# A macaron block on one Trainium2 core: max scores three steps further from their transpose, exponentials four steps later, two of twelve runs joined

## The chip, the cores and the metric

One core of one Trainium2 chip runs the whole program. The core has a matrix engine (TensorE, PE in the profile; PEld is its loading of weights), a vector engine (VectorE, DVE), a scalar engine (ScalarE, ACT), a general engine (GpSimd, POOL) and a queue that issues transfers (SyncE, SP). The metric is the device time of one execution in microseconds, and the median of three runs is compared.

## The reference

Two batches of 1024 tokens with 512 channels pass through half a feed-forward layer with ternary weights, an attention layer of 16 heads of width 32, and half a feed-forward layer again:

```python
x = x + 0.5 * _L0_ffn_ref(_layernorm(x, axis=-1), weight, bias, ln_gamma, ln_beta)
x = x + _L0_attn_ref(_layernorm(x, axis=-1), w_q, w_k, w_v, w_o)
x = x + 0.5 * _L0_ffn_ref(_layernorm(x, axis=-1), weight, bias, ln_gamma, ln_beta)
# attention, for each head: q and k with rotary embedding
scores = where(mask, q @ k.T * SCALE, -inf)     # causal in blocks of 64, in effect
ctx = softmax(scores) @ v
out = ctx @ w_o.T
```

With a dilation of one block every block at or before the query's is allowed, so the mask is causal in blocks of 64.

## The kernel before

The 16 heads of a batch are taken four at a time, so that there are 8 groups of four heads (`ALL`). The middle of the kernel is one long list of steps `k`, and every engine runs the same list in its own order of instructions. 48 steps (`STEPS`) belong to one group, 12 steps (`A_UNITS`) to one head. In a step TensorE issues, in this order, at most:

- one exponential's score product (L920, "B unit"): keys on the partitions, one of 12 key steps (`st`, called key step below) of one of the four heads. Key step 0 to 3 have 512, 384, 256, 128 columns, 4 to 8 have 512, and 9 to 11 have 384, 256, 128. ScalarE takes the exponential of it into `probs` (L609), which has room for four key steps. There are two banks for B units, so that B unit u waits until the exponential of u-2 is done (L919).
- one max product (L939, "A unit"): queries on the partitions, one of 12 units of a head, number 0 to 11, with 128, 256, 384, 512, 512, 128, 512, 256, 512, 384, 512, 512 columns. VectorE reduces it to its maximum (L815). There are three banks, so that an A unit waits until the reduction of the unit three before it is done (L937).
- one or two of the 12 projection products of a later group (L956): at k mod 12 from 0 to 9, two of them at 4 and at 9, none at 10 and 11. After them ScalarE copies the projection out (L602, at k mod 12 = 10), GpSimd turns it by the rotary angles in four instructions (two at L502, then L505 and L507), ScalarE makes the high half (L623, eight steps after the projection's last), GpSimd the low half (L511), and SP writes both out to `spread` and reads them back into `qst` or `kst` (L398 to L409). In the last groups output products (L884) and the second feed-forward layer (L864 to L874) stand in their place, in the first the values' products (L993).
- where k mod 4 is 3, a "run": four products with ones (L1045, the sums of the exponentials of one key step, five steps behind its first B unit, `SUM_LAG`) and four with the values (L1055, the key step before that one, nine steps behind, `PV_LAG`), in fp32 and in four parts of the array side by side.
- once a head the transpose of the head's max parts (L1063).

When the last A unit of a head (number 11) is reduced, VectorE makes the "max parts" of the head in three small instructions, each waiting for the one before: L825 takes the smaller of two columns sets, L827 a scaled fp16 copy, L828 what the copy leaves out. L1063 transposes them on TensorE `MAX_PLACE` steps after unit 11, in a bank of the three A banks (`max_bank`), ScalarE copies the result one step later (L617), and SP writes it into `qst` two steps later (L414). The next A unit of that bank waits for the copy (`s_mrows`, L933), and the two before it wait one unit deeper (L935). With `A_START` = 10 unit 0 stands at k mod 12 = 10 and unit 11 at 9, and the transpose at 11, behind the run there. With `B_START` = 18 the key steps of a group begin at k mod 48 = 18, and its runs stand at 23 for the sums of key step 0 up to 67 for those of key step 11.

At the end of a half (key step 3 or 11) ScalarE takes the logarithm and the reciprocal of the sums (L629, L633), VectorE multiplies (L834), ScalarE and GpSimd split the context into its halves (L641, L521). The last of these (L521 of group 7) opens the output products of the second batch's upper rows (wait at L1069).

The VectorE part of a step, in its order:

```python
if t := a_unit(k):
    nc.vector.tensor_reduce(rmax[:, at:at + 1], a_bank(u)[:, 0:n], AX.X, ALU.max, negate=True)   # L815
if e := max_head(k, 0):
    link(nc.vector.tensor_tensor(rmax[...], rmax[...], rmax[...], ALU.min))                      # L825
    link(nc.vector.tensor_scalar(mparts[:, s, 0, :], rmax[...], 1.0 / MAX_SCALE, None, ALU.mult)) # L827
    nc.vector.scalar_tensor_tensor(mparts[:, s, 1, :], rmax[...], 1.0 / MAX_SCALE, mparts[:, s, 0, :], ...)  # L828
```

Of the kernel before, what the change touches and what calls it, by code (L numbers as in the profile page):

```python
# [30 lines left out]
GH = P // D  # L31
# [16 lines left out]

STEPS = 48
ALL = BATCH * GROUPS  # L50
A_START, B_START = 10, 18
SUM_LAG, PV_LAG = 5, 9
P_PLACES = 4

SLOTS = [(0,), (1,), (2,), (3,), (4, 5), (6,), (7,), (8,), (9,), (10, 11)]
MAX_PLACE = 2
A_ORDER = [(i, half) for i in range(TILES) for half in range(i // 4 + 1)]
A_UNITS = len(A_ORDER)
B_ORDER = [(half, j) for half in range(BLOCKS) for j in range(4 * half + 4)]
# [7 lines left out]
def macaron(nc, x, w_q, w_k, w_v, w_o, w_f, bias, gamma, beta, cos_t, sin_t, ident_in, ident16_in,  # L67
            q_rows, k_rows, spread, out):
    ctx = ExitStack()
    with ctx:  # L70
# [139 lines left out]
        s_max = sem("s_max")  # L210
# [26 lines left out]
        def proj_unit(k, lag=0):  # L237

            g, r = divmod(k - lag, STEPS)
            if 0 <= g < ALL and r % A_UNITS < len(SLOTS):  # L240
                return g, r // A_UNITS, r % A_UNITS

        def proj_after(k, lag):

            u = proj_unit(k, lag)
            return u[:2] if u and u[2] == len(SLOTS) - 1 else None

# [24 lines left out]
        def a_bank(u):  # L272

            return pa[(u + max(0, (u - MAX_PLACE) // A_UNITS)) % 3]

        def max_bank(n):

            return pa[(A_UNITS * (n + 1) + MAX_PLACE + n) % 3]

        def max_head(k, lag):  # L280

            t = a_unit(k - lag)
            return t[:2] if t and t[2:] == A_ORDER[-1] else None
# [9 lines left out]
        def pv_step(k, lag):  # L293

            t = b_unit(k - lag)
            return (t[0], t[1], *t[3:]) if t and t[2] == 0 else None

        def ctx_half(k, lag=1):

            s = pv_step(k - lag, PV_LAG)  # L300
            return (s[0], s[2]) if s and s[3] == 4 * s[2] + 3 else None
# [21 lines left out]
        def _(sp):  # L323
# [64 lines left out]
            for k in range(LAST_STEP):  # L388
                if u := proj_after(k, 11):
                    g, m = u  # L390
                    n = 4 * g + m
                    sp.wait_ge(s_rl, n + 1)
                    if n >= 2:
                        g2, m2 = divmod(n - 2, 4)
                        sp.wait_ge(s_stack[m2], (g2 + 1) * 16)

                    low, again = (slice(0, 3, 2), 1) if m % 2 else (slice(0, 2), 2)
                    sp.dma_start(spread[n % 2, low].rearrange("a p t -> p a t"), rhl[:, n % 2, :, :]  # L398
                                 ).then_inc(s_spread[n % 2], 16)
                    sp.dma_start(spread[n % 2, again], rhl[:, n % 2, 0, :]).then_inc(s_spread[n % 2], 16)  # L400
                if u := proj_after(k, 14):
                    g, m = u
                    n = 4 * g + m
                    dst, cols = (kst if m % 2 else qst), slice(m // 2 * HALF, (m // 2 + 1) * HALF)
                    sp.wait_ge(s_spread[n % 2], (n // 2 + 1) * 32)
                    if g >= SETS:
                        sp.wait_ge(s_qb, STEPS * (g - SETS + 1))
                    sp.dma_start(dst[0:MASK_ROW, g % SETS, :, cols],
                                 spread[n % 2].rearrange("a (d h) t -> (a d) h t", h=GH)).then_inc(s_stack[m], 16)  # L409
                if e := max_head(k, 4):  # L410
                    g, h = e
                    n = GH * g + h
                    sp.wait_ge(s_mrows, n + 1)
                    sp.dma_start(qst[MAX_ROW:ROWS_B, g % SETS, h, :], mrows[:, n % 2, :]).then_inc(s_mdma[h], 16)  # L414
                for bl in range(BLOCKS):
                    if k == F1_STEP[4 * bl + 3] + 6:
                        residual_out(1, bl)
                    if k == STEPS + 16 + 6 * bl:
                        columns_out(bl)
                    if k == STEPS * 3 + 24 + 24 * bl:  # L420
                        columns_in(bl)
                    if k == STEPS * 7 + 24 + 24 * bl:
                        context_in(bl)
                if k == STEPS + 10:
                    sp.wait_ge(s_wl, 4)
                    sp.wait_ge(s_xtr[1], 8)
                    mask_rows(1, SETS)
                if k in CTX_STEPS:
                    context_out(CTX_STEPS.index(k))
                if k == CTX_STEPS[3] + 2:  # L430
                    sp.wait_ge(s_pv, 12 * GROUPS)
                    for bl in range(BLOCKS):
                        sp.wait_ge(s_x1out[bl][0], 16)
                        sp.dma_start(resid[0][bl], x1_dram[0][:, 4 * bl:4 * bl + 4, :]).then_inc(s_x1in[0], 16)
                if k == B_END - STEPS + 4:
                    sp.wait_ge(s_qb, STEPS * 7)
                    for bl in range(BLOCKS):
                        sp.wait_ge(s_x1out[bl][1], 16)
                        sp.dma_start(resid[1][bl], x1_dram[1][:, 4 * bl:4 * bl + 4, :]).then_inc(s_x1in[1], 16)
                if k - 7 in F3_STEP:  # L440
                    store(0, F3_STEP.index(k - 7))
# [86 lines left out]
        def _(act):  # L528
# [52 lines left out]
            for k in range(LAST_STEP):  # L581
# [15 lines left out]
                if u := proj_after(k, 1):  # L597
                    n = 4 * u[0] + u[1]
# [4 lines left out]
                if t := b_unit(k):  # L603
                    g, st, h, half, j, q0, n = t
                    u = STEPS * g + GH * st + h
                    act.wait_ge(s_qb, u + 1)
                    if 12 * g + st >= P_PLACES:
                        act.wait_ge(s_pv, 12 * g + st + 1 - P_PLACES)
                    nc.scalar.activation(probs[:, st % P_PLACES, h, 0:n], pb[u % 2][:, 0:n], ACT.Exp,  # L609
                                         scale=EXP_SCALE).then_inc(s_eb, 1)  # L610
                if e := max_head(k, 3):
                    n = GH * e[0] + e[1]
                    act.wait_ge(s_mtr, n + 1)
                    if n >= 2:
                        g2, h2 = divmod(n - 2, GH)
                        act.wait_ge(s_mdma[h2], (g2 + 1) * 16)
                    nc.scalar.activation(mrows[:, n % 2, :], max_bank(n)[0:2 * TILES, 0:P // 2].bitcast(F16), ACT.Copy).then_inc(s_mrows, 1)  # L617
                if u := proj_after(k, 8):
                    n = 4 * u[0] + u[1]
# [4 lines left out]
                if c := ctx_half(k, -4):  # L624
                    n = 2 * c[0] + c[1]
# [4 lines left out]
                if c := ctx_half(k, 0):  # L630
                    n = 2 * c[0] + c[1]
# [223 lines left out]
        def _(pe):  # L855
# [52 lines left out]
            for k in range(LAST_STEP):  # L908
# [4 lines left out]
                if t := b_unit(k):  # L913
                    g, st, h, half, j, q0, n = t
# [7 lines left out]
                if t := a_unit(k):  # L922
# [15 lines left out]
                    n = min(HALF, (i + 1) * P - half * HALF)  # L938
# [3 lines left out]
                if u := proj_unit(k):  # L942
# [9 lines left out]
                    og = g % GROUPS  # L952
                    for n in SLOTS[i]:
                        a, cc = divmod(n, CC)
# [73 lines left out]
                if p := product_part(F3_STEP, k):  # L1028
# [3 lines left out]
                        if r % 4 >= 2:  # L1032
                            pe.wait_ge(s_up3[0], r - 1)
                    product(f3_bank[0][r], r, xh, xl, THIRDS[i], s_ffn3[0])
                if t := pv_step(k, SUM_LAG):
                    g, st, half, j, q0, n = t
                    pe.wait_ge(s_eb, STEPS * g + GH * (st + 1))
                    if st == 0 and g % GROUPS == 0:
                        pe.wait_ge(s_vs[g // GROUPS], TILES)
                    if j == 0 and (g or half):  # L1040
                        pe.wait_ge(s_ln, 2 * g + half)
                    if g == 0 and st == 0:
                        pe.wait_ge(s_vs[1], TILES)
                    for h in range(GH):
                        last = nc.tensor.matmul(psum[h * D:(h + 1) * D, q0 - half * HALF:HALF], ones[:, 0:D],  # L1045
                                                probs[:, st % P_PLACES, h, 0:n], start=(j == 0), stop=(j == 4 * half + 3),
                                                skip_group_check=True)
                    last.then_inc(s_sum, 1)
                if t := pv_step(k, PV_LAG):
                    g, st, half, j, q0, n = t  # L1050
                    if j == 0 and (g or half):
                        pe.wait_ge(s_cf, 2 * g + half)
                    og = g % GROUPS
                    for h in range(GH):
                        last = nc.tensor.matmul(acc[h * D:(h + 1) * D, q0 - half * HALF:HALF],  # L1055
                                                rows[g // GROUPS][:, j, (GH * og + h) * D:(GH * og + h + 1) * D],
                                                probs[:, st % P_PLACES, h, 0:n], start=(j == 0), stop=(j == 4 * half + 3),
                                                skip_group_check=True)
                    last.then_inc(s_pv, 1)
                if e := max_head(k, MAX_PLACE):  # L1060
                    n = GH * e[0] + e[1]
                    pe.wait_ge(s_mp, n + 1)
                    nc.tensor.transpose(max_bank(n)[0:2 * TILES, 0:P // 2].bitcast(F16),  # L1063
                                        mparts[:, n % 2, :, :].rearrange("p a t -> p (a t)"),
                                        ident16[:, :]).then_inc(s_mtr, 1)
# [87 lines left out]
```

## Time and profile before

| | us |
|---|---|
| median of 3 runs | 634.64 (634.29 to 636.09) |
| the profiled execution's own time | 634.23 |
| its span, first to last instruction | 632.4 |
| TensorE busy | 554.8 (88%) |
| VectorE busy | 396.8 (63%) |
| ScalarE busy | 310.2 (49%) |
| GpSimd busy | 238.5 (38%) |
| mean granted TensorE clock | 0.962 |

TensorE is busy for most of the span, and in the steady part its clock is granted in full. The busy share alone doesn't say what a change is worth: what counts is where TensorE stands still, and which engine it then waits for. The steady part is the stretch from about 190 to 470 us, where a group takes 47.2 to 47.4 us.

### The profile page before, as it was taken

What the parts mean: (1) busy time and instruction counts of PE and PEld (TensorE: products, weight loads), DVE (VectorE), ACT (ScalarE), POOL (GpSimd) and SP (SyncE); (2) the same over time, 40 slices, a digit from 0 to 9 for tenths busy, and PEclk for the clock granted to TensorE, in tenths of its full rate; (3) what the DMA queues carried; (4) which work ended last, traced back from release to release, by engine and by line L of the source; (5) the groups of instructions that cost most, each with busy time, mean ns of one, the idle gap of its engine ahead of it and who ended that gap; (6) DMA issues with size and microseconds to landing.
All of it is one profiled execution on the core that took longest, in us unless ns stands there. A gap on an engine that the chain in (4) does not pass through costs nothing.

```text
span 632.4 us, 10042 instructions
## 1 busy us (share of the span) xinstructions
PE 554.8 (88%) x3586; PEld 235.9 (37%) x3586; DVE 396.8 (63%) x782; ACT 310.2 (49%) x629; POOL 238.5 (38%) x200
## 2 busy tenths in 40 slices
PE   0695799679969999999999999999999898999876
PEld 0442445334423333333333333333333334344432
DVE  5899656626767757757757657657657843431672
ACT  0931632121215746746746746746736548572320
POOL 4001363443474646646646646646600100000100
PEclk9796899888989999999999999999999999999997
DMA  8921023354221215423213214514410003100011
GB/s 322 348 76 68 2 70 97 117 119 133 93 83 51 77 52 175 127 67 110 76 51 109 77 52 150 169 51 143 138 57 2 1 2 134 51 18 34 33 68 66
DMA packets 43601, 57.95 MB, mean 92 GB/s; under 512 B 3526, under 2 KB 34374, under 8 KB 42528
## 3 DMA queue, kind: packets, MB, share of 16 engines
q1 hardware_dynamic: 42972, 57.21, 27.6%
q8 instruction: 29, 0.48, 0.3%
q10 hardware_dynamic: 580, 0.11, 0.1%
q14 instruction: 20, 0.16, 0.1%
HBM read 32.01 MB, written 25.17 MB: 90 GB/s over the span
## 4 chain that ended last, share of the span: by engine, by line
PE 56%; DVE 19%; issue 8%; POOL 7%; DMA 7%; ACT 3%; SPq 1%; ACTq 0%; POOLq 0%; DVEq 0%
PE bank L956 9%; PE bank L874 7%; PE bank L939 7%; PE bank L920 7%; PE bank L1045 6%; PE bank L1055 5%; PE bank L884 5%; PE bank L993 5%; DMA kst<-spread 4%; DVE rmax L815 4%; DVE mparts L828 3%; DVE stats L661 3%; POOL rot L502 2%; DMA spread<-rhl 2%; PE bank L864 2%
## 5 line engine op out<-in xcount | busy, mean ns | idle before, releaser
L815 DVE TENSOR_REDUCE rmax<-bank 128x1 f32<-128x512 f32 (+3 forms) x384 | 200.9, 553 | 124.5 <-PE bank L939 121.5
L609 ACT ACTIVATE big<-bank 128x512 f32<-128x512 f32 (+3 forms) x384 | 182.0, 490 | 150.6 <-PE bank L920 145.7
L939 PE MATMUL bank<-kst,qst 104*128 104x512 f16 (+3 forms) x384 | 126.3, 330 | 15.3 <-issue 8.5
L920 PE MATMUL bank<-qst,kst 106*128 106x512 f16 (+3 forms) x384 | 123.9, 330 | 2.5 <-ACT big L609 2.2
L502 POOL TENSOR_TENSOR rot<-t,sin_s 64x512 f32<-64x512 f32 x64 | 81.8, 1277 | 96.3 <-ACT t L602 93.5
L1045 PE MATMUL bank<-big,ones 128*32 128x512 f32 (+3 forms) x768 | 81.8, 498 | 0.0
L1055 PE MATMUL bank<-big,rows 128*32 128x512 f32 (+3 forms) x768 | 79.5, 486 | 0.0
L920 PEld LDWEIGHTS bank<-qst,kst 106*128 106x128 f16 x384 | 37.1, 97 | 84.4 <-issue 41.4
L511 POOL TENSOR_TENSOR rhl<-t,rhl 128x512 f16<-128x512 f32 x32 | 37.5, 1171 | 70.9 <-ACT rhl L623 70.9
L521 POOL TENSOR_TENSOR cl<-cf,ch 128x512 f16<-128x512 f32 x16 | 18.6, 1160 | 112.3 <-ACT ch L641 112.3
L939 PEld LDWEIGHTS bank<-kst,qst 104*128 104x128 f16 x384 | 37.8, 98 | 51.2 <-issue 18.9
L956 PE MATMUL bank<-xh,wh 128*128 128x512 f16 x128 | 50.9, 401 | 6.4 <-DVE xl L697 5.9
L956 PE MATMUL bank<-xl,wh 128*128 128x512 f16 x128 | 44.9, 392 | 0.0
L461 POOL TENSOR_TENSOR rstd<-var_e,half_neg 128x4 f32<-128x4 f32 x12 | 13.0, 1084 | 83.5 <-DVE var_e L670 83.5
L956 PE MATMUL bank<-xh,wl 128*128 128x512 f16 x128 | 43.6, 381 | 0.0
L507 POOL TENSOR_TENSOR t<-t,rot 128x512 f32<-128x512 f32 x32 | 41.2, 1286 | 2.5
L505 POOL TENSOR_TENSOR t<-t,cos_s 128x512 f32<-128x512 f32 x32 | 40.9, 1280 | 2.5
L1055 PEld LDWEIGHTS bank<-big,rows 128*32 128x32 f32 x768 | 24.5, 110 | 37.5 <-issue 34.7
L690 DVE SCALAR_TENSOR_TENSOR rows<-bank,rows 128x512 f32<-128x512 f32 x24 | 16.3, 689 | 35.0 <-PE bank L874 34.8
L543 ACT ACTIVATE xh<-bank,bet,gam 128x512 f16<-128x512 f32 x24 | 18.9, 787 | 35.9 <-PE bank L864 35.9
L828 DVE SCALAR_TENSOR_TENSOR mparts<-rmax,mparts 128x8 f16<-128x8 f32 x32 | 34.6, 1081 | 1.1
L623 ACT ACTIVATE rhl<-t 128x512 f16<-128x512 f32 x32 | 20.0, 626 | 20.5 <-POOL t L507 20.5
(106 smaller groups left out, 667.9 us busy)
## 6 DMA issues: line engine op xcount, KB each, us to landing
spread<-rhl SPq DMA_DIRECT2D x32, 256.0 KB, 2.2
qst<-spread SPq DMA_DIRECT2D x16, 384.0 KB, 3.8
kst<-spread SPq DMA_DIRECT2D x16, 384.0 KB, 3.8
x<-rows SPq DMA_DIRECT2D x4, 1024.0 KB, 4.6
spread<-rhl SPq DMA_DIRECT2D x32, 128.0 KB, 2.1
rows<-in_L_attn_x_dram SPq DMA_DIRECT2D x3, 1024.0 KB, 15.5
xh<-ch SPq DMA_DIRECT2D x4, 512.0 KB, 4.6
xl<-cl SPq DMA_DIRECT2D x4, 512.0 KB, 6.2
```

The lines of the kernel that those rows point to most:

```text
L502: pool.tensor_tensor(rot[first:first + P // 2, n % 2, :], t1[other:other + P // 2, n % 2, :], sin_s[other:other + P // 2, cols], ALU.mult) ...
L505: pool.tensor_tensor(t1[:, n % 2, :], t1[:, n % 2, :], cos_s[:, cols], ALU.mult).then_inc(s_rot, 1)
L507: pool.tensor_tensor(t1[:, n % 2, :], t1[:, n % 2, :], rot[:, n % 2, :], ALU.add).then_inc(s_rope, 1)
L609: nc.scalar.activation(probs[:, st % P_PLACES, h, 0:n], pb[u % 2][:, 0:n], ACT.Exp, scale=EXP_SCALE).then_inc(s_eb, 1)
L815: nc.vector.tensor_reduce(rmax[:, at:at + 1], a_bank(u)[:, 0:n], AX.X, ALU.max, negate=True).then_inc(s_max, 1)
L828: nc.vector.scalar_tensor_tensor(mparts[:, s, 1, :], rmax[:, at:at + 8], 1.0 / MAX_SCALE, mparts[:, s, 0, :], ALU.mult, ALU.subtract).then ...
L874: last = nc.tensor.matmul(dst[:, :], (high, low)[a][:, cc, r * P:(r + 1) * P], wt[:, cc, :], start=False, stop=(n == 2 * CC))
L920: nc.tensor.matmul(pb[u % 2][:, 0:n], kst[0:ROWS_B, g % SETS, h, j * P:(j + 1) * P], qst[0:ROWS_B, g % SETS, h, q0:q0 + n], start=True, st ...
L939: nc.tensor.matmul(a_bank(u)[:, 0:n], qst[0:ROWS_A, g % SETS, h, i * P:(i + 1) * P], kst[0:ROWS_A, g % SETS, h, half * HALF:half * HALF + ...
L956: last = nc.tensor.matmul(pp[:, :], wp[ww][:, m % 2, cc, og * P:(og + 1) * P], xp[xw][:, cc, m // 2 * HALF:(m // 2 + 1) * HALF], start=(n ...
L1045: last = nc.tensor.matmul(psum[h * D:(h + 1) * D, q0 - half * HALF:HALF], ones[:, 0:D], probs[:, st % P_PLACES, h, 0:n], start=(j == 0), s ...
L1055: last = nc.tensor.matmul(acc[h * D:(h + 1) * D, q0 - half * HALF:HALF], rows[g // GROUPS][:, j, (GH * og + h) * D:(GH * og + h + 1) * D], ...
```

## The change

`A_START` goes from 10 to 11 and `B_START` from 18 to 22: every max product stands one step later, every B unit and with it every sum, value product and context step four steps later, while the projections stay. `MAX_PLACE` goes from 2 to 5: the transpose of the max parts, its copy and its transfer stand three steps further behind the head's last A unit, and the bank that the transpose takes lies between units 4 and 5 of the next head, not between 1 and 2. A wait for the reduction of the unit that held that bank is added. The sums of key step 2 (and 10) are not issued in their own place but in front of those of key step 3 (11), and the values of key step 1 (9) in front of those of key step 2 (10), which is the same place: of the twelve runs of a group the one at the sums of key step 2 (10) is left empty, and the next holds 16 products.

```diff
-A_START, B_START = 10, 18
+A_START, B_START = 11, 22
 SUM_LAG, PV_LAG = 5, 9
 P_PLACES = 4
 
+MERGED = (2, 10)
+
-MAX_PLACE = 2
+MAX_PLACE = 5
...
+        def sums_of(k):
+
+            s = pv_step(k, SUM_LAG)
+            if not s or s[1] in MERGED:
+                return []
+            return [pv_step(k - GH, SUM_LAG), s] if s[1] - 1 in MERGED else [s]
+
+        def values_of(k):
+
+            s = pv_step(k, PV_LAG)
+            if not s or s[1] + 1 in MERGED:
+                return []
+            return [pv_step(k - GH, PV_LAG), s] if s[1] in MERGED else [s]
...
-                if e := max_head(k, 4):
+                if e := max_head(k, MAX_PLACE + 2):
...
-                if e := max_head(k, 3):
+                if e := max_head(k, MAX_PLACE + 1):
...
-                if t := pv_step(k, SUM_LAG):
+                for t in sums_of(k):
...
-                if t := pv_step(k, PV_LAG):
+                for t in values_of(k):
...
                 if e := max_head(k, MAX_PLACE):
                     n = GH * e[0] + e[1]
                     pe.wait_ge(s_mp, n + 1)
+                    if n + 1 < GH * ALL:
+                        pe.wait_ge(s_max, A_UNITS * (n + 1) + MAX_PLACE - 2)
                     nc.tensor.transpose(max_bank(n)[0:2 * TILES, 0:P // 2].bitcast(F16),
```

## Rows read from the trace of the kernel before

**Rows 1.** Busy time by stretch (us, then each engine with its instruction count, granted clock):
```profile
333.97:381.19 47.22, 45.54 (x341) 17.89 (x340) 32.02 (x62) 29.56 (x67) 27.22 (x22) 1.00 0.25 79
```

**Rows 2.** Waits of TensorE, 190 to 480 us (us in total, times, longest):
```profile
PE bank L1063 <- DVE mparts L828: 6.4, 12, 0.7
PE bank L939 <- DMA kst<-spread: 4.7, 6, 1.0
```

**Rows 3.** Waits of TensorE, 130 to 190 us:
```profile
PE bank L939 <- issue: 8.5, 2, 4.7
PE bank L1063 <- DVE mparts L828: 3.5, 4, 1.8
```

**Rows 4.** Timeline (start us, us, engine): TensorE around one full run:
```profile
354.33 0.38 PE L956 MATMUL bank<-xh,wl 128*128 128x512 f16 x1
354.63 1.07 PE L1045 MATMUL bank<-big,ones 128*32 128x512 f32 x8
355.52 1.04 PE L1055 MATMUL bank<-big,rows 128*32 128x512 f32 x8
356.49 0.39 PE L920 MATMUL bank<-qst,kst 106*128 106x512 f16 x1
```

**Rows 5.** Timeline of TensorE: end of the run of key steps 3 and 2, transpose:
```profile
346.70 0.61 PE L1055 MATMUL bank<-big,rows 128*32 128x256 f32 x8
347.98 0.22 PE L1063 MATMUL bank<-ident,mparts 128*16 128x128 f16 x1 [0.67 <-DVE mparts L828]
```

**Rows 6.** Timeline of all engines at a head's end, 333 to 338 us:
```profile
333.56 0.38 PE L939 MATMUL bank<-kst,qst 104*128 104x512 f16 x1
...
333.97 1.35 DVE L815 TENSOR_REDUCE rmax<-bank 128x1 f32<-128x512 f32 x2 [0.99 <-PE bank L939]
...
334.43 0.59 PE L956 MATMUL bank<-xh,wl 128*128 128x512 f16 x2
...
335.06 0.60 ACT L602 ACTIVATE t<-bank 128x512 f32<-128x512 f32 x1
...
335.74 2.62 POOL L502 TENSOR_TENSOR rot<-t,sin_s 64x512 f32<-64x512 f32 x2 [2.65 <-ACT t L602]
335.76 1.28 DVE L828 SCALAR_TENSOR_TENSOR mparts<-rmax,mparts 128x8 f16<-128x8 f32 x1
...
337.09 1.26 POOL L502 TENSOR_TENSOR rot<-t,sin_s 64x512 f32<-64x512 f32 x1
```

**Rows 7.** Timeline: VectorE instructions with SBUF inputs beside GpSimd's:
```profile
74.49 3.11 POOL L502 TENSOR_TENSOR rot<-t,sin_s 64x512 f32<-64x512 f32 x2 [7.93 <-ACT t L602]
...
77.12 1.03 DVE L684 TENSOR_TENSOR cl<-big,ch 128x512 f16<-128x512 f32 x1 [0.65 <-ACT big L544]
...
117.37 1.60 DVE L676 TENSOR_SCALAR kst<-rows,mv,rstd 128x512 f32<-128x512 f32 x1 [1.21 <-POOL rstd L461]
```

**Rows 8.** Timeline: max parts of the first batch's fourth head:
```profile
179.96 0.17 DVE L827 TENSOR_SCALAR mparts<-rmax 128x8 f16<-128x8 f32 x1
179.98 2.61 POOL L502 TENSOR_TENSOR rot<-t,sin_s 64x512 f32<-64x512 f32 x2
```

**Rows 9.** Groups by line and shape (busy us, mean ns of one, idle before):
```profile
L815 DVE TENSOR_REDUCE rmax<-bank 128x1 f32<-128x512 f32 x192 | 129.5, 689 | 108.9 <-PE bank L939 107.2
L815 DVE TENSOR_REDUCE rmax<-bank 128x1 f32<-128x128 f32 x64 | 18.0, 281 | 3.8 <-PE bank L939 3.7
L623 ACT ACTIVATE rhl<-t 128x512 f16<-128x512 f32 x32 | 20.0, 626 | 20.5 <-POOL t L507 20.5
```

**Rows 10.** One line's instructions (duration ns min/median/max): the fp32 to fp16 comparison at L718, and L828:
```profile
L718 DVE TENSOR_SCALAR xl<-cl,sums x1: 1286/1286/1286, 18.5 to 18.5; 128x2048 f16<-128x2048 f32 x1
...
L828 DVE SCALAR_TENSOR_TENSOR mparts<-rmax,mparts x32: 168/1278/1290, 151.2 to 516.7; 128x8 f16<-128x8 f32 x32
```

**Rows 11.** Timeline at the end of the last run:
```profile
585.42 0.43 PE L1055 MATMUL bank<-big,rows 128*32 128x128 f32 x8
...
588.72 1.04 PE L884 MATMUL bank<-wh,ch 128*128 128x512 f16 x4 [1.47 <-POOL cl L521]
```

## The prediction

> **What bounds the kernel now.** I read the granted clock and the busy times by stretch first. In a steady group of 47.2 us TensorE is busy for 45.5 us at full clock, VectorE for 32.0, ScalarE for 29.6 and GpSimd for 27.2 [rows 1]: TensorE bounds, and only its standing still or its switching can be saved. The waits of TensorE say where it stands still. From 190 to 480 us it waits 12 times for L828 before the transpose L1063, 6.4 us together, and 6 times for the transfer into `kst`, 4.7 us [rows 2]. Before that stretch it waits 3.5 us for L828 and twice, 8.5 us together, with no releaser shown ("issue") [rows 3]; by their place these two are the same `kst` wait at unit 4 in groups 0 and 1. Last I read the timeline around a run and around a head's end, since the change moves these against each other.
>
> A product of 512 columns takes 0.22 us from start to start (354.33 to 354.63 is that and 0.08 for entering the run), and in proportion fewer columns take less. A full run lasts from 354.63 to 356.49, 1.86 us; its halves have 4 x 512 columns, 0.85 us each, so that some 0.04 lies between the halves and 0.12 behind the second [rows 4]. With the entry that is 0.24 us a run beyond its columns.
>
> **The head's end in VectorE is not what it seems.** L828 works on 8 elements and takes 1.28 us, though it can take 0.17 [rows 10]. It starts at 335.76, 0.02 behind the first of GpSimd's L502 (335.74), and ends at 337.04, where that one ends, since the second starts at 337.09 [rows 6]. So a VectorE instruction with two SBUF inputs is held while a GpSimd instruction runs. It is so in mid-instruction too: L684, 0.69 us when alone by its neighbours, starts at 77.12 inside an L502 that ends at 77.60 and takes 1.03 [rows 7]. A tensor-scalar is held as well: L676 took 1.60 us [rows 7]. L827, which started 0.02 before GpSimd, took its 0.17 [rows 8]. Today only L828 meets GpSimd.
>
> **What the change removes.**
> 1. Behind a short run the transpose now waits, by 0.67 us in the case shown [rows 5]. It will come five steps and a run behind unit 11 instead of two steps. All waits for L828 at L1063 go: 6.4 us in the steady part [rows 2]. The 3.5 us of group 0 [rows 3] come back otherwise (below).
> 2. The wait for `kst` at unit 4: the projection whose transfer is awaited keeps its place, and unit 4 comes one step later. From the projection's end to unit 4 TensorE then has one unit of 512 columns more, 512 of projection, some 1400 of B units and 512 of the run at k mod 48 = 11: 2940 columns, 1.2 us, less a transpose. The longest wait is 1.0 us, so 4.7 us go [rows 2]. In groups 0 and 1 the wait stays, and one step's projection and value products (0.65 and 0.22 us) move in front of it: 0.9 us.
> 3. Each joined run saves an entry and an exit, 0.09 + 0.12 us [rows 4]. 16 joins: 3.3 us. If fp32 products of another kind behind each other pay the switch all the same, it is 0 to 3.3.
> Sum: 6.4 + 4.7 + 0.9 + 3.3 = 15.3 us.
>
> **What it adds.** Name s the time when the B unit of k mod 12 = 10 starts. L602 starts at the end of the last projection product, and L502 0.72 us behind that end (334.43 + 0.59 to 335.74) [rows 6], which is s + 0.88. Unit 11 used to stand a step earlier, so that L828 met GpSimd's start; now it stands at the step of s. It starts at s + 0.22, VectorE begins 0.41 later (333.56 to 333.97) [rows 6] and takes 0.69 [rows 9]: L825 wants to start at s + 1.35, in the middle of the first L502, and is held to s + 2.18. L827 then starts about 0.04 later, 0.02 ahead of the second L502, as in [rows 8], and gets through; L828 comes 0.2 behind it and is held until the second L502 ends, s + 3.53. The max parts take 2.2 us instead of 1.7. The reduction of the next head's unit 0 follows (0.28) [rows 9], and unit 3, which needs unit 0's bank, can start at s + 3.79. Who feels it depends on what TensorE has between s and unit 3:
> - Where a full run stands at k mod 12 = 11 (k mod 48 = 10, 22, 46; at 22 the run behind it is the joined one), TensorE comes to unit 3 at s + 3.73, s + 4.0 and s + 4.0: 0.06 us for one head of 7 groups, 0.4.
> - At k mod 48 = 34 the run is the one that the join empties. B units have 128 columns, there is no projection for two steps, and TensorE would be at unit 3 at s + 1.46. It waits 2.33 us. Six groups have this head with projections: 14.0 us. In the seventh there is no GpSimd work, but VectorE still has 0.69 twice and the max parts for steps of 0.1 to 0.3 us: 0.9.
> - The first head of group 1 (k = 118) has no run yet, B units of 512, unit 3 at s + 2.1: 1.7.
> - Group 0 has no runs: three heads wait 0.63 for the bank where they waited 0.58 for the transpose; the fourth is absorbed by the `kst` wait behind it.
> Queued behind the waiting A unit are that step's projection product and the next B unit, so ScalarE starves too, but has slack.
> The other edits: the copy L617 now stands next to L623, 0.63 us [rows 9], on ScalarE, and may hold B units of 128 columns by 0.1 us a group (0 to 0.3): 0.7 for 7 groups. The added wait asks for a reduction at least three steps old and costs nothing behind a run. SP's transfer of the max rows and B units both keep eight steps between them. In the tail the last value run comes four steps later, behind the last feed-forward products. After the last run at 585.42 (0.36 us) these covered what TensorE now waits 1.47 for beside [rows 11]: 588.72 - 1.47 - 585.78 = 1.5 us of cover, gone.
> Sum: 0.4 + 14.0 + 0.9 + 1.7 + 0.7 + 1.5 = 19.2 us.
>
> **The result** is 634.23 + 19.2 - 15.3 = 638.1 for the profiled execution, whose time is 0.4 below the median of the three, so 638.5 us.
>
> The Trainium skill (SBUF — State Buffer, section "SBUF: two separate sides") says that the port pair shared by VectorE and GpSimd is an exclusive lock held for the whole instruction, against VectorE instructions with two SBUF inputs or in a two-port mode. By that rule the change walks its three small instructions into GpSimd's row, which speaks against it; [rows 6, 7] agree. The Trainium skill (VectorE: DVE Perf Modes, section "The perf-mode tier table") gives such a mode to a tensor-scalar from fp32; L718, 2048 elements from fp32 to fp16 in 1286 ns [rows 10], fits it. That leaves L827 open to be held too, the second rival.
>
> **Rivals.**
> A. *The three instructions get by.* If L825 and L827 are so short that they aren't held, L828 ends with the first L502, s + 2.18, and unit 3 may start at s + 2.44: the 14.0 become 6 x 0.98 = 5.9, the 1.7 become 0.3, and group 0 loses its 1.9: 638.5 - 11.7 = 626.8. If they are held but all slip into the gap behind the first L502, unit 3 starts at s + 2.95: 630.4. For it: nothing in the trace shows an instruction of 4 elements held. Against it: L828 has 8 elements and is held each time. Chance 0.22.
> B. *L827 loses the race.* It starts 0.02 before the second L502, a margin that one row carries [rows 8]. If it is held by it and L828 by L505 behind it, the max parts end 1.34 us later, in all heads: the stalls grow by 1.34 for k mod 48 = 10 and 34, by 1.1 for 22 and 46, 4.9 us a group. 6 groups, group 1's first head and three heads of group 0: 35 us, 673 us. This decides as soon as the gap is lost in most heads. Chance 0.12.
> C. *The savings don't come.* The joins bring nothing and the `kst` wait only moves, because SP waits for L617 of an earlier head before it issues: 638.5 + 8.0 = 646. Against it: the order of these waits on SP stays the same up to three steps. Chance 0.10.
> D. *The terms cancel.* Gains and losses are 15 and 19 us, and an error of a fifth in the 14.0, or a VectorE less behind than I count, leaves 634 to 636. Chance 0.13.
>
> **How the numbers follow.** My forecast, 638.5 with 636.6 to 643 around it, has 0.43. A measurement of this kernel tells 0.3%, 1.9 us, from no change. Faster is A and a little of D: 0.25. Same is most of D, 632.7 to 636.5: 0.15. Slower is the forecast, B, C: 0.60. The range leaves out B and the lower end of A: 629 to 647, about 0.8. Cases of both signs hold weight; the likeliest one's own range is 636.6 to 643.
>
> **What would show it.** In the changed kernel's profile: L1063 waits for L828 nowhere in the steady part (1); the `kst` wait is under 1 us in total (2); the joined run lasts 1.9 us for 4096 columns in each of its four parts of the array (3). L825 and L828 both take over 0.8 us on average where projections run, L827 0.17. L939 waits for L815 six to seven times by 2 to 2.5 us, once a group, in front of the joined run of key steps 2 and 3. A group takes about 47.4 us. If L825 shows 0.16, rival A holds; if L827 shows 1.3, rival B. The prediction is wrong if the long wait is not at that head, or if the runs' absence there costs nothing.

## The result: 642.9 us, 1.3% slower

| | before | after |
|---|---|---|
| median | 634.46 us (4 runs) | 642.88 us (640.26 to 642.94, 4 runs) |
| ratio to before | | 1.0126 (1.0107 to 1.0146) |
| profiled execution, its span | 634.23, 632.4 | 642.83, 641.0 |
| TensorE busy | 554.8 (88%) | 557.2 (87%) |
| VectorE busy | 396.8 | 409.1 |
| mean granted TensorE clock | 0.962 | 0.965 |

In the new file L815 has become L831, L825/L827/L828 are L841/L843/L844, L502/L521 of GpSimd are L518/L537, L920 and L939 are L936 and L955, the runs are L1061 and L1071, and L884 is L900. These are TensorE's waits after, from 190 to 480 us and then from 130 to 190 us (us in total, times, longest); they answer to [rows 2, 3]:

```profile
PE bank L955 <- DVE rmax L831: 10.5, 8, 1.5
PE bank L936 <- ACT big L625: 3.3, 7, 0.6
PE bank L955 <- DMA kst<-spread: 0.4, 1, 0.4
...
PE bank L955 <- issue: 6.2, 2, 3.9
PE bank L955 <- DVE rmax L831: 4.5, 6, 1.7
```

The transpose waits for nothing any more and the `kst` wait is down from 4.7 us to 0.4. In their place the max product L955 waits for reductions, and the exponentials' product L936 for ScalarE. One head's end where the run is empty (k mod 48 = 34), all engines; the first line is that of VectorE's reductions of the head's last two units:

```profile
296.83 1.40 DVE L831 TENSOR_REDUCE rmax<-bank 128x1 f32<-128x512 f32 x2
297.94 2.61 POOL L518 TENSOR_TENSOR rot<-t,sin_s 64x512 f32<-64x512 f32 x2 [1.74 <-ACT t L618]
298.26 0.96 DVE L841 TENSOR_TENSOR rmax<-rmax 128x4 f32<-128x4 f32 x1
299.26 0.17 DVE L843 TENSOR_SCALAR mparts<-rmax 128x8 f16<-128x8 f32 x1
299.46 1.11 DVE L844 SCALAR_TENSOR_TENSOR mparts<-rmax,mparts 128x8 f16<-128x8 f32 x1
300.50 0.61 DVE L831 TENSOR_REDUCE rmax<-bank 128x1 f32<-128x128 f32 x2
```

L841 works on four elements and takes 0.96 us: it starts 0.32 behind GpSimd's first L518 and ends with it. L843 slips into the gap, 0.17. L844 ends at 300.57, with the second L518 (300.55). Only then is unit 0 reduced, whose bank unit 3 needs. What TensorE does meanwhile and afterwards:

```profile
298.08 0.23 PE L936 MATMUL bank<-qst,kst 106*128 106x128 f16 x1 [0.46 <-ACT big L625]
...
298.92 0.38 PE L936 MATMUL bank<-qst,kst 106*128 106x512 f16 x1
300.83 0.61 PE L955 MATMUL bank<-kst,qst 104*128 104x512 f16 x1 [1.53 <-DVE rmax L831]
301.24 0.63 PE L972 MATMUL bank<-xh,wh 128*128 128x512 f16 x1
301.66 0.63 PE L936 MATMUL bank<-qst,kst 106*128 106x512 f16 x1
302.09 0.63 PE L955 MATMUL bank<-kst,qst 104*128 104x512 f16 x1
```

It waits 0.46 and then 1.53 us, and behind the wait products of 512 columns start 0.43 us apart where they had started 0.22 apart [rows 4]: the engine is at 1.2 GHz. By stretch (us, busy times of the engines, then clock, DMA share, GB/s), three groups of the new kernel from one such head to the next:

```profile
204.35:251.31 46.96, 44.97 (x343) 18.00 (x341) 33.71 (x63) 29.86 (x66) 27.26 (x23) 1.00 0.32 99
251.31:298.26 46.95, 44.96 (x342) 18.00 (x340) 33.71 (x62) 29.86 (x66) 27.24 (x23) 1.00 0.33 103
298.26:346.76 48.50, 46.50 (x343) 18.34 (x341) 33.81 (x63) 29.86 (x66) 27.24 (x23) 0.96 0.24 77
```

A group at full clock takes 46.95 us, 0.3 less than before [rows 1]; the group with the low clock takes 1.55 more. The second such fall is at 444 us. And the tail, where the last value run no longer has feed-forward products behind it:

```profile
591.65 0.43 PE L1071 MATMUL bank<-big,rows 128*32 128x128 f32 x8
595.59 1.89 PE L900 MATMUL bank<-wh,ch 128*128 128x512 f16 x4 [3.52 <-POOL cl L537]
597.27 1.91 PE L900 MATMUL bank<-wh,cl 128*128 128x512 f16 x4
598.98 1.91 PE L900 MATMUL bank<-wl,ch 128*128 128x512 f16 x4
600.69 1.21 PE L900 MATMUL bank<-wh,ch 128*128 128x512 f16 x4
601.73 1.03 PE L900 MATMUL bank<-wh,cl 128*128 128x512 f16 x4
```

The wait for L537 is 3.52 us instead of 1.47 [rows 11], and the first twelve products behind it take 1.7 us per four, not 0.87: 2.5 us more, again at 1.2 GHz. Some 0.8 of it comes back: the next stretch at 1.2 GHz, which both kernels have near their end, lasts 3.4 us here (from 628 us) and 6.8 before (from 617 us), and from the product behind L537 to the end are 45.4 us, against 43.7 before. The low clock of the tail costs 1.7 us net.

**Where the 8.6 us of the two profiles are.** Gone: waits of the transpose 9.9 and for `kst` 4.3, "issue" 2.3 [rows 2, 3], and, as estimated, 3.3 for 16 joins: 19.8. Come: waits for reductions, 17.8 after against 2.0 before over the whole span, 15.8; for ScalarE at L936, 5.3 against 2.2, 3.1; for L537 2.0; a new wait for a normalization in the tail, 1.0; low clock in the steady part 1.55 twice, 3.1, and in the tail 1.7; and 0.9 that the two profiles differ by at 74 us, ahead of all that was changed. Together 27.6. The difference is 7.8, and the spans show 8.6: 0.8 us are not assigned, and the 3.3 for the joins is an estimate.

### The profile page after: what moved, and what is told of

Same layout as the page of the kernel before. It is cut to its first block, busy times and chain, and to the rows that moved or that the text cites. A ratio compares the mean times of both kernels' runs of the same rounds, so it can differ in the third digit from the quotient of the medians.

```text
span 641.0 us, 10072 instructions
## 1 busy us (share of the span) xinstructions
PE 557.2 (87%) x3586; PEld 239.2 (37%) x3586; DVE 409.1 (64%) x782; ACT 312.3 (49%) x629; POOL 238.8 (37%) x200
## 4 chain that ended last, share of the span: by engine, by line
PE 69%; DVE 20%; issue 3%; DMA 2%; POOL 2%; ACT 2%; SPq 0%; ACTq 0%; DVEq 0%; POOLq 0%
PE bank L972 11%; PE bank L1061 10%; PE bank L936 9%; PE bank L1071 9%; PE bank L955 9%; PE bank L890 7%; PE bank L900 6%; PE bank L1009 5%; DVE rmax L831 4%; DVE stats L677 3%; PE bank L880 2%; DVE mparts L844 2%; DVE big L692 2%; DVE rmax L841 2%; DVE kst L692 1%
## 5 line engine op out<-in xcount | busy, mean ns | idle before, releaser
L831 DVE TENSOR_REDUCE rmax<-bank 128x1 f32<-128x512 f32 (+3 forms) x384 | 198.2, 551 | 114.1 <-PE bank L955 111.8
L955 PE MATMUL bank<-kst,qst 104*128 104x512 f16 (+3 forms) x384 | 126.9, 333 | 24.6 <-DVE rmax L831 17.8
L936 PE MATMUL bank<-qst,kst 106*128 106x512 f16 (+3 forms) x384 | 126.2, 330 | 5.6 <-ACT big L625 5.3
L518 POOL TENSOR_TENSOR rot<-t,sin_s 64x512 f32<-64x512 f32 x64 | 82.0, 1281 | 86.7 <-ACT t L618 84.0
L1061 PE MATMUL bank<-big,ones 128*32 128x512 f32 (+3 forms) x768 | 79.6, 503 | 0.0
L1071 PE MATMUL bank<-big,rows 128*32 128x512 f32 (+3 forms) x768 | 76.7, 486 | 0.0
L936 PEld LDWEIGHTS bank<-qst,kst 106*128 106x128 f16 x384 | 37.0, 97 | 85.2 <-issue 32.8
L955 PEld LDWEIGHTS bank<-kst,qst 104*128 104x128 f16 x384 | 38.0, 99 | 65.6 <-DVE rmax L831 23.4
L537 POOL TENSOR_TENSOR cl<-cf,ch 128x512 f16<-128x512 f32 x16 | 18.8, 1178 | 93.3 <-ACT ch L657 93.3
L972 PE MATMUL bank<-xh,wl 128*128 128x512 f16 x128 | 44.2, 385 | 0.0
L521 POOL TENSOR_TENSOR t<-t,cos_s 128x512 f32<-128x512 f32 x32 | 40.9, 1279 | 2.5
L1071 PEld LDWEIGHTS bank<-big,rows 128*32 128x32 f32 x768 | 24.6, 111 | 41.0 <-issue 40.7
L618 ACT ACTIVATE t<-bank 128x512 f32<-128x512 f32 x32 | 19.1, 597 | 27.7 <-PE bank L972 27.1
L844 DVE SCALAR_TENSOR_TENSOR mparts<-rmax,mparts 128x8 f16<-128x8 f32 x32 | 30.9, 965 | 1.1
## 6 DMA issues: line engine op xcount, KB each, us to landing
rows<-in_L_attn_x_dram SPq DMA_DIRECT2D x3, 1024.0 KB, 15.8
```

What stands on the lines that cost most here:

```text
L518: pool.tensor_tensor(rot[first:first + P // 2, n % 2, :], t1[other:other + P // 2, n % 2, :], sin_s[other:other + P // 2, cols], ALU.mult) ...
L521: pool.tensor_tensor(t1[:, n % 2, :], t1[:, n % 2, :], cos_s[:, cols], ALU.mult).then_inc(s_rot, 1)
L844: nc.vector.scalar_tensor_tensor(mparts[:, s, 1, :], rmax[:, at:at + 8], 1.0 / MAX_SCALE, mparts[:, s, 0, :], ALU.mult, ALU.subtract).then ...
L936: nc.tensor.matmul(pb[u % 2][:, 0:n], kst[0:ROWS_B, g % SETS, h, j * P:(j + 1) * P], qst[0:ROWS_B, g % SETS, h, q0:q0 + n], start=True, st ...
L955: nc.tensor.matmul(a_bank(u)[:, 0:n], qst[0:ROWS_A, g % SETS, h, i * P:(i + 1) * P], kst[0:ROWS_A, g % SETS, h, half * HALF:half * HALF + ...
L972: last = nc.tensor.matmul(pp[:, :], wp[ww][:, m % 2, cc, og * P:(og + 1) * P], xp[xw][:, cc, m // 2 * HALF:(m // 2 + 1) * HALF], start=(n ...
```

## The experiments

My theory has three parts: (a) the max parts meet two GpSimd instructions, each of which holds VectorE's; (b) this costs where the run behind a head's end is empty; (c) the tail loses its cover. The rivals are that a later place, an empty run or VectorE's backlog cost by themselves, or that all of it is the tail. Every ratio is to the kernel before in the same session (medians 634.35, 635.53 and 635.18 us in the three), given with its 95% interval. "Per group" is the time between the same steps of two successive groups in the steady part, 47.3 us before.

**The joins alone**, everything in its old place:

```diff
+MERGED = (2, 10)
 # with sums_of and values_of of the change; A_START, B_START = 10, 18 and MAX_PLACE = 2 kept
```

> The kernel before with the two joins of runs alone; max products, exponentials and transpose in their old places. My theory: the empty runs are then at k mod 48 = 31 and 15, before the head's end and not behind it, so that VectorE keeps up; 16 joins save 3.3 us and the short run that left the transpose waiting becomes a long one, 3 to 4 us more: 628 to 631 us. Rival (an empty run costs wherever it is, as VectorE and ScalarE fall behind in seven steps): 636 to 642.

628.09 us, ratio 0.9886 (0.9844 to 0.9928), 46.0 us per group: as expected. The wait of the transpose falls from 6.4 to 2.3 us, since the run in front of it is now a long one:

```profile
PE bank L955 <- DMA kst<-spread: 4.6, 6, 1.1
PE bank L1081 <- DVE mparts L844: 2.3, 6, 0.6
```

So an empty run costs nothing in its old place, where no max product waits for VectorE in the steady part; where it stands decides.

**The changed kernel without joins:**

```diff
-MERGED = (2, 10)
+MERGED = ()
```

> The changed kernel with no run joined (all twelve in their places), the rest as changed. My theory: the wait of unit 3 at k mod 48 = 34 shrinks from 2.0 to about 1.1 us, one of 0.8 us comes at k mod 48 = 22, where the run is short again, the clock doesn't fall behind shorter stalls (3 us back), and 3.3 us of entries and exits return: 641 to 644 us. Rival (the loss is the tail, the joins are a plain gain): 646.

637.62 us, ratio 1.0050 (1.0034 to 1.0066), 46.9 us per group. It is faster than the changed kernel, whose joins therefore lose about 5 us where they gain 6 in the old places. The rival "a plain gain" falls. It is 3.4 us below my range: unit 3 waits 0.85 us at k mod 48 = 34 and 0.64 at 22, not 1.1 and 0.8. The groups at full clock take the same time with and without joins (46.9). Of the 5.0 us between the two profiles 3.1 are the clock, which doesn't fall here in the steady part, and 1.2 lie in the first group with an emptied run, which takes 44.2 us with the joins and 43.0 without, from one projection copy (171 us) to the one four further on; the rest I haven't assigned.

**The changed kernel with one of the joins**, that of key step 10, so that the run behind the head's end at 34 is filled:

```diff
-MERGED = (2, 10)
+MERGED = (10,)
```

> The changed kernel with only the sums of key step 10 joined (MERGED = (10,)), so that the run at k mod 48 = 35, behind the head's end at 34, is filled again. My theory: the wait of unit 3 there shrinks from 2.0 us (1.5 for VectorE, 0.5 for ScalarE) to about 1.1 us in six groups, the clock stays at 2.4 GHz, and 1.6 us of entries and exits return: 635 to 638 us. Rival (the tail is the loss): 644.5. If the stall is not replaced at all and only the clock recovers: 640.

631.38 us, ratio 0.9937 (0.9918 to 0.9955), 45.9 us per group, and no low clock in the steady part. This is 3.6 us below what I expected: the join at 22 gives 1.0 us per group against no join. 0.64 of it is unit 3's wait; the other 0.33 is more than the 0.21 of an entry and exit that I had counted. Its steady waits:

```profile
PE bank L955 <- DVE rmax L831: 6.4, 8, 0.9
PE bank L936 <- ACT big L625: 0.6, 1, 0.6
```

This shows (b): one emptied run of two turns a kernel that is 0.6% faster into one that is 1.3% slower.

**Without the meeting of VectorE and GpSimd**, in the changed kernel. GpSimd waits for the max parts before it starts the rotation:

```diff
                     pool.wait_ge(s_rstd, roots)
+                    if n >= 5:
+                        pool.wait_ge(s_mp, n - 4)
```

> The changed kernel with one wait more: GpSimd starts a projection's rotation only when the max parts of the head that ends one step earlier are written. VectorE's three small instructions then meet no GpSimd instruction and should take 0.17 us each. My theory (SBUF instructions of VectorE are held by GpSimd's): the max parts end 1.6 us earlier, the wait of unit 3 at k mod 48 = 34 shrinks from 2.0 to about 0.8 us, those of groups 0 and 1 go, and the clock doesn't fall: 629 to 633 us. Rival (the stall is VectorE's plain backlog of reductions, or the wait on GpSimd delays the rotation and the transfer to kst): 641 to 645.

625.61 us, ratio 0.9861 (0.9827 to 0.9896), 45.1 us per group, 3.4 us below my range. This is the test of (a): no VectorE instruction was changed, and the three of them now take 0.17 us each. In its lines the reduction is L833, the max parts L843/L845/L846, the rotation L520:

```profile
290.98 0.16 DVE L843 TENSOR_TENSOR rmax<-rmax 128x4 f32<-128x4 f32 x1
291.18 0.17 DVE L845 TENSOR_SCALAR mparts<-rmax 128x8 f16<-128x8 f32 x1
291.38 0.17 DVE L846 SCALAR_TENSOR_TENSOR mparts<-rmax,mparts 128x8 f16<-128x8 f32 x1
291.81 2.63 POOL L520 TENSOR_TENSOR rot<-t,sin_s 64x512 f32<-64x512 f32 x2 [2.90 <-DVE mparts L846]
```

The waits for reductions in the steady part fall from 10.5 us to 0.5, lower than the 0.8 a group that I had left, the clock stays up there, and the change as a whole turns from 1.3% slower to 1.4% faster. The later start of the rotation costs nothing in the steady part, since the `kst` transfer has its new slack; in groups 0 and 1 the "issue" waits grow from 6.2 to 9.7 us. VectorE's backlog of reductions was not the cause. The Trainium skill (SBUF — State Buffer, section "SBUF: two separate sides") says that the port pair shared by VectorE and GpSimd is an exclusive lock held for a whole instruction. The traces agree: L841 and L844 took 0.96 and 1.11 us beside the rotation, and take 0.17 with the rotation behind them.

**The same wait in the kernel before:**

> The kernel before with the same added wait on GpSimd. My theory: L828 takes 0.17 us instead of 1.28, the transposes' waits for it (9.9 us in all) go, the rotation starts 0.2 us later and the kst wait grows by about that in six groups: 625 to 629 us. Rival (L828 takes its time for another reason): 634 or more, and L828 still at 1.1 us or more.

626.04 us, ratio 0.9857 (0.9833 to 0.9880). The time is within my range, the transpose no longer waits in the steady part, and the `kst` wait grows from 4.7 to 6.0 us, all as expected. L828 was expensive only for whom it met.

**Both remedies** in the changed kernel, MERGED = (10,) and GpSimd's wait:

> The changed kernel with both remedies: only key step 10 joined, and GpSimd waiting for the max parts. My theory: unit 3 waits nowhere in the steady part; against the changed kernel 10.5 us of these waits, 2 to 3 us of low clock, 3 us in groups 0 and 1 go, and 1.6 us of joins return: 626 to 630 us. If the two remedies cure the same thing: no better than the better one of them alone.

624.96 us, ratio 0.9832 (0.9803 to 0.9860). It is 1 us below my 626 to 630, and only 0.3% from the wait alone, with overlapping intervals, which is what I had written for two remedies of one thing. Without the meeting, the empty run costs little more than ScalarE's 0.46 us per group (45.1 against 44.7 us per group). The two remedies cure mostly the same thing.

**The lowest time**: the kernel before with both joins and GpSimd's wait, nothing shifted:

> The kernel before with the two joins and the wait of GpSimd for the max parts, nothing shifted. The joins alone gave 628.1, the wait alone 626.0. If both gains add where they don't overlap (3.3 us of entries and exits for the joins; about 8 us of waits at the transpose for the other): 621.5 to 624 us. Rival (the joins gain by hiding the same transpose waits only): 626.

622.13 us, ratio 0.9813 (0.9778 to 0.9848), as expected and the lowest of all, 1.9% less than before; its interval overlaps that of the version above, so that which of the two is faster is not shown. In a group it is behind that one (45.5 against 44.7 us) because of its `kst` wait, 5.6 us in the steady part; it gains in the tail, where the wait for the last context is 1.47 and not 3.52 us, at full clock behind it.

**The transpose's place alone**, five steps behind, nothing else:

```diff
-MAX_PLACE = 2
+MAX_PLACE = 5
 # A_START, B_START = 10, 18 and no joins kept
```

> The kernel before with the transpose of the max parts five steps behind a head's last max product (MAX_PLACE 5, with its added wait) and nothing else moved; runs not joined. My theory (the loss comes from unit 3 of the max products, held by the three small VectorE instructions that are held by GpSimd, at the head where a run is empty): here VectorE's part stays where it was and every run is in its place, so the transpose's waits, 6 to 10 us, go and nothing replaces them: 626 to 629 us. Rival 1 (the later place itself costs, by bank turns around units 5 to 7): 634 or more. Rival 2 (the tail of the later exponentials is the loss) also expects 626 to 629.

634.82 us, ratio 1.0007 (0.9989 to 1.0025). Of the expectations only rival 1's number held, and its reason is a part of the truth. The waits for L828, 9.9 us, are gone, but the time isn't. The max products' waits for reductions are 6.7 us over the whole span instead of 2.0 (1.9 in the steady part, where there were none), and the `kst` wait is 5.9 instead of 4.7. And TensorE is busy for 560.3 us instead of 554.8. The reason that I see for this in its timeline is where the transpose L1081 stands, in the middle of products and not behind a run:

```profile
339.68 0.38 PE L972 MATMUL bank<-xh,wh 128*128 128x512 f16 x1
339.99 0.22 PE L1081 MATMUL bank<-ident,mparts 128*16 128x128 f16 x1
340.15 0.28 PE L936 MATMUL bank<-qst,kst 106*128 106x256 f16 x1
```

From 339.68 to 340.15 are 0.47 us, of which the product takes 0.22: 0.25 for the transpose. Behind a run it costs almost nothing, since the run's exit of 0.12 is paid anyway: in the changed kernel as in [rows 4] the next product comes 0.97 behind the start of L1071's 512 columns, and with a transpose between them 1.01 (268.44 to 269.45). In this run 30 of the 32 transposes stand like this one, with 0.46 or 0.47 us around them. 0.2 us for each of 32 is 6.4 us, about the 5.5 that TensorE is busier. With the 4.7 and 1.2 of waits that came this is 11.4, a little more than the 9.9 that went. This working is from the traces, not an experiment of its own. The change itself keeps the transpose behind a run, so that it doesn't pay this.

**The shift alone**, A_START 11 and B_START 22:

> The kernel before with the shift alone (A_START 11, B_START 22), transpose two steps behind unit 11, no joins. My theory: VectorE's three small instructions now meet two of GpSimd's and end 0.8 us later against the projection while the transpose is only one step later, so the transpose waits in every head, 0.4 to 1.5 us, about 3.7 us a group instead of 1.0, and the tail costs 3: 645 to 650 us. Rival (the port has no part in it; the shift is neutral but for the tail): 636 to 638.

650.86 us, ratio 1.0246 (1.0222 to 1.0269), 49.1 us per group, 0.9 us above what I expected. The transpose two steps behind unit 11 waits in nearly every head:

```profile
PE bank L1081 <- DVE mparts L844: 18.4, 22, 1.4
```

**The exponentials' shift alone**, for the tail:

```diff
-A_START, B_START = 10, 18
+A_START, B_START = 10, 22
```

> The kernel before with the exponentials alone four steps later (B_START 22); max products and transpose as before, no joins. This measures the tail: the last value run then stands behind the feed-forward products. From the changed kernel's trace I expect the wait for L521 to be 3.5 us instead of 1.5, and the output products behind it to run at 1.2 GHz for about 5 us, which costs 2.5 us more; the transposes' waits stay near 6 us: 638.5 to 640 us. Rival (the tail costs only its cover, 1.5 us, and the rest of the loss lies in the steady part): 636.

650.59 us, ratio 1.0241 (1.0194 to 1.0288): far above both expectations, so that this run doesn't isolate the tail. Its wait for L521 is 3.5 us, as expected, but the transpose's wait is 15.2 us where I had said "near 6". The context's L834 moves with the exponentials, to the place one unit ahead of a head's end, and pushes the max parts back by its 0.68 us:

```profile
266.66 0.68 DVE L834 SCALAR_TENSOR_TENSOR cf<-bank,cf 128x512 f32<-128x512 f32 x1
267.25 0.68 DVE L815 TENSOR_REDUCE rmax<-bank 128x1 f32<-128x512 f32 x1
267.81 2.63 POOL L502 TENSOR_TENSOR rot<-t,sin_s 64x512 f32<-64x512 f32 x2 [2.75 <-ACT t L602]
267.97 1.14 DVE L825 TENSOR_TENSOR rmax<-rmax 128x4 f32<-128x4 f32 x1
269.15 0.17 DVE L827 TENSOR_SCALAR mparts<-rmax 128x8 f16<-128x8 f32 x1
269.35 1.11 DVE L828 SCALAR_TENSOR_TENSOR mparts<-rmax,mparts 128x8 f16<-128x8 f32 x1
```

L825 starts 0.16 behind GpSimd and is held, L828 after it: the same loss by another way, 0.96 us at that transpose. Six heads have it, which waited nothing before: 5.8 us of the 8.9 that the transposes wait more over the whole span. The rest of the 15 us I haven't taken apart.

**The tail of the changed kernel, covered again:**

```diff
-        Y3_STEP = [...] + [O0_START + 97 + 2 * n for n in range(4)]
-        F3_STEP = [...] + [O0_START + 107 + 4 * r for r in range(4)]
+        Y3_STEP = [...] + [O0_START + 101 + 2 * n for n in range(4)]
+        F3_STEP = [...] + [O0_START + 111 + 4 * r for r in range(4)]
```

> The changed kernel with the second block of the last transposes and feed-forward products of batch 0 (Y3_STEP 97 to 101, F3_STEP 107 to 111, in steps behind O0_START) four steps later, so that it follows the last value run again. My theory: the wait for L521 returns to 1.5 us and the products behind it stay at 2.4 GHz: 4 to 4.5 us less than the changed kernel, 638.5 us. Rival (the clock falls there anyway, or the products now end later than the chain): 641 to 643.

637.79 us, ratio 1.0039 (1.0022 to 1.0055), as expected, and the wait is back at 1.47 us with the products behind it at full clock:

```profile
592.49 1.04 PE L900 MATMUL bank<-wh,ch 128*128 128x512 f16 x4 [1.47 <-POOL cl L537]
```

The changed kernel took 642.45 us in the same session (below), so that the tail was 4.7 us of its 7.3 behind the kernel before. The trace gives the same: 2.0 of wait, 1.7 of clock net, and 1.0 of the wait for a normalization, which is gone too. This shows (c).

**The changed kernel once more**, for the clock:

> The changed kernel once more, for the clock: in its first profile products of 512 columns took 0.63 us and not 0.38 for some microseconds behind two of the six waits of 1.5 us, and its four times were 642.9 three times and 640.3 once. If the fall of the clock belongs to these long waits, this profile shows it behind one to four of them again, and nowhere else in the steady part; the median is 640 to 643 us.

642.45 us, ratio 1.0111 (1.0074 to 1.0149), as expected. The clock falls behind two of six such waits again, but not the same two: at 301 and 397 us here, at 301 and 444 in the first profile. Behind the steady part it falls here also after the wait of 1.78 us at 502 us, which it didn't in the first profile.

```profile
301.04 0.61 PE L955 MATMUL bank<-kst,qst 104*128 104x512 f16 x1 [1.52 <-DVE rmax L831]
301.44 0.63 PE L972 MATMUL bank<-xh,wh 128*128 128x512 f16 x1
```

## Why the prediction was right, and what was mis-sized

The forecast was slower, 638.5 us in a range of 629 to 647; measured are 642.9. The direction and the mechanism held, the loss was twice what I had worked out (8.4 against 4).

- *L825 held by the first rotation, L827 through the gap, L828 held by the second*: right in every head of the steady part, 0.68 to 0.96, 0.17 and 1.11 us. The race that rival B rested on is won in all 27 heads that meet the rotation. From s (297.06) to unit 3 (300.83) are 3.77 us; I had 3.79.
- *The head at k mod 48 = 34*: right. 1.53 and 0.46 us of waits, 1.99, where I had 2.33.
- *All the stalls behind reductions and ScalarE*: 15.8 + 3.1 us against 19.6 that I had (17.7 in the sum and 1.9 for group 0's heads). Right in size.
- *Savings*: transpose and `kst` waits went as forecast. The joined run takes 1.87 us from its start to the next product (239.27 to 241.14), 0.16 beyond its columns' 1.71, as a single run does (1.86 for 1.71, [rows 4]). A group at full clock less its waits for reductions and ScalarE is 45.4 us without joins and 45.0 with two, 0.2 a join: the 3.3 us stand, and nothing speaks for rival C. The "issue" waits gave 2.3 us instead of 0.9.
- *The tail*: this term was mis-sized. I had 1.5 us for the lost cover. It was 2.0 of wait, 1.0 for the normalization, and 1.7 of low clock. The wait is longer than the cover because L850 starts late: VectorE's two updates in front of it begin 0.3 us ahead of the run's end, and 0.9 ahead in the kernel before.

VectorE in the changed kernel's tail; the last value run ends at 592.0, and L850 starts 0.95 behind it, where it was 0.3 before:

```profile
591.75 0.69 DVE L706 SCALAR_TENSOR_TENSOR rows<-bank,rows 128x512 f32<-128x512 f32 x1 [4.95 <-PE bank L890]
592.36 0.68 DVE L720 SCALAR_TENSOR_TENSOR qst<-bank,qst 128x512 f32<-128x512 f32 x1
592.96 0.68 DVE L850 SCALAR_TENSOR_TENSOR cf<-bank,cf 128x512 f32<-128x512 f32 x1
```

- *The clock*: not in the sum at all. I counted a wait as its own length. Behind 1.5 us of standing still, two in six cost 1.55 us more. Both clock terms together are 4.8 us, more than the whole gap of 4.4 to the forecast; the smaller errors roughly cancel.
- Rival A (the small instructions aren't held) is refuted by the rows, rival D by the ratio.
- *The prediction's own arithmetic*: rival A's terms (8.1, 1.4 and 1.9) add up to 11.4 and not 11.7, and the forecast, B and C to a chance of 0.65 where "slower" has 0.60. Neither changes the forecast.

What would have shown it wrong, a long wait at another head or an empty run without cost, holds only in half: the empty run costs nothing in the old place.

## What to carry to other kernels

Here VectorE instructions of four to eight elements took 0.58 to 1.29 us, not 0.17, when they met a GpSimd instruction of 1.3 us, and in a chain of three two were held, so look at who runs beside such a chain before calling it cheap or dear. One wait that orders the two engines was worth 1.4% here; the two joins alone gave 1.1% and the shift alone cost 2.5%. When work is shifted on one engine of several, list again what each moved instruction now meets, its followers too (the context step met the head's end here). And price a wait of TensorE with the slower products behind it, as well as its length.

## What the runs showed of the hardware that I had not expected

- TensorE went to 1.2 GHz behind a wait of 1.5 us, though it had been busy for over 95% of the group before; in each of three profiles of the changed kernel's steady part (the two of the changed kernel and that with the tail covered) it did so in two of six equal waits, and not in the same two each time, and stayed there for 3.4 us (products 0.43 us apart). Which waits it would be I can't tell beforehand. Behind the wait of 3.5 us in the tail it did so in seven of eight profiles; in the eighth, the shift alone, the products behind it took 0.87 us per four, full clock, and the end came 43.8 us behind the wait, not 45.4. Behind the 1.47 us of the tail it didn't in any of six.
- A transpose with 16 columns of weights costs 0.25 us between other products, and 0.04 behind a run in four parts of the array.
- Between GpSimd's two L518 there is a gap of about 0.09 us (335.74 + 1.26 to 337.09 in the kernel before). L843 started in it, 0.02 ahead of the second, in all 27 heads that meet the rotation and took its 0.17; L844, 0.2 later, was held each time.
- L827, the tensor-scalar, can be held too. In the run with the exponentials' shift alone it started once 0.08 us behind a GpSimd instruction (L521 at 511.85) and took 1.09 us.
